# Attention's four engine queues written in another order, in a two-layer transformer kernel on one core

## What is computed

```python
def _L0_attn_ref(x, Wq, Wk, Wv, Wo, gn_weight, gn_bias):       # 8 heads of width 16
    qT, kT, vT = (proj(Wq), proj(Wk), proj(Wv))
    def step(S, qkv_t):
        q_t, k_t, v_t = qkv_t
        S = g * S + k_t[..., :, None] * v_t[..., None, :]      # g: one decay for each head
        y_t = jnp.einsum('bhde,bhd->bhe', S, q_t)
        return (S, y_t)
    ...
    out = (out - mean) * jax.lax.rsqrt(var + EPS)              # group norm over time and head width
    out = out.reshape(B, L, D) * gn_weight + gn_bias
    return out @ Wo.T

h = _layernorm(x, axis=-1) * (1 + ca) + sa
x = x + ga * _L0_attn_ref(h, ...)
h = _layernorm(x, axis=-1) * (1 + cb) + sb
scores = jnp.einsum('BTC,CE->BTE', h, gate_w)                  # logits of the feed-forward's router
probs = jax.nn.softmax(scores, axis=-1)
```

## Time and profile before

| what | value |
|---|---|
| median of 3 runs | 1448.95 us (1447.45 to 1464.47) |
| the profiled execution's own time | 1469.19 us |
| its span, first to last instruction | 1467.0 us |
| PE busy | 1130.1 us (77% of the span) |
| DVE busy | 893.7 us (61%) |
| ACT busy | 687.8 us (47%) |
| POOL busy | 561.8 us (38%) |
| mean granted TensorE clock | 0.859 |

### The profile page before, as it was taken

One profiled execution on the slowest core, in us unless ns is written; L12 is line 12 of the kernel. 1 busy time (PEld: TensorE's weight loads), 2 busy tenths in 40 slices (PEclk: granted clock), 3 DMA queues, 4 the chain that ended last, 5 costly groups with the idle time before them and its releaser, 6 DMA issues. The chain is left out here.

```text
span 1467.0 us, 23954 instructions
## 1 busy us (share of the span) xinstructions
PE 1130.1 (77%) x6776; PEld 857.3 (58%) x6777; DVE 893.7 (61%) x1786; ACT 687.8 (47%) x1527; POOL 561.8 (38%) x882
## 2 busy tenths in 40 slices
PE   2887885689978688888888888883374799999860
PEld 1555554334448578777888877773243666666640
DVE  2355553711039599999999999993376633333327
ACT  1334432233324587888778887771241033333320
POOL 1000000300012277777877778770000155555540
PEclk9667775799989789999999999996555599999995
DMA  6000000011010200000000000002310011111115
GB/s 181 0 1 1 0 1 1 0 44 43 29 29 0 58 1 1 1 0 0 0 0 0 0 0 0 0 0 90 97 33 17 6 35 39 36 39 38 38 48 181
DMA packets 41607, 39.87 MB, mean 27 GB/s; under 512 B 4041, under 2 KB 37474, under 8 KB 41202
## 3 DMA queue, kind: packets, MB, share of 16 engines
q1 hardware_dynamic: 32466, 22.37, 5.2%
q0 software_dynamic: 4608, 9.45, 2.3%
q10 hardware_dynamic: 4496, 7.60, 1.5%
HBM read 30.44 MB, written 8.96 MB: 27 GB/s over the span
## 5 line engine op out<-in xcount | busy, mean ns | idle before, releaser
L1181 DVE TENSOR_TENSOR_SCAN s_hs<-s_dA,bank 128x1024 f32<-128x1024 f32 x128 | 291.9, 2280 | 10.2 <-PE bank L1532 10.1
L1409 POOL TENSOR_SCALAR s_dbuT<-s_dtuT,s_BT 128x256 f32<-128x256 f32 x512 | 239.9, 492 | 11.0 <-ACT s_dtuT L1264 8.8
L1292 ACT ACTIVATE s_dA<-s_dt,aneg 128x255 f32<-128x255 f32 x512 | 213.6, 498 | 0.6 <-DVE s_hs L1181 0.4
L1982 POOL DMA_INDIRECT x_xg<-hf_rows,x_src x72 | 69.7, 968 | 236.9 <-issue 170.6
L1532 PE MATMUL bank<-const,s_dbuT 128*128 128x128 f32 x1024 | 139.7, 282 | 26.0 <-POOL s_dbuT L1409 26.0
L1189 DVE TENSOR_TENSOR s_hc<-s_hs,bank 128x1024 f32<-128x1024 f32 x128 | 156.1, 1220 | 5.2 <-PE bank L1520 0.9
L2022 PE MATMUL bank<-w,x_xT 128*128 x288 | 128.4, 569 | 19.0 <-ACT x_xT L2064 16.3
L1550 PE MATMUL bank<-const,s_hc 128*128 128x128 f32 x1024 | 138.0, 280 | 2.2 <-DVE s_hc L1189 2.2
L1532 PEld LDWEIGHTS bank<-const,s_dbuT 128*128 128x128 f32 x1024 | 119.8, 145 | 32.7 <-issue 26.3
L1550 PEld LDWEIGHTS bank<-const,s_hc 128*128 128x128 f32 x1024 | 120.7, 145 | 2.4 <-DVE s_hc L1189 2.4
L2060 ACT ACTIVATE x_a<-bank 128x448 f32<-128x448 f32 x72 | 39.1, 543 | 161.6 <-PE bank L2022 156.7
(11 more groups left out here) (301 smaller groups left out, 2273.6 us busy)
## 6 DMA issues: line engine op xcount, KB each, us to landing
w<-in_w SPq DMA_DIRECT2D x16, 256.0 KB, 3.1
o_yr<-y_rows SPq DMA_DIRECT2D x8, 512.0 KB, 3.9
w<-in_w ACTq DMA_DIRECT2D x1, 3584.0 KB, 13.3
x_res<-in_x SPq DMA_DIRECT2D x4, 512.0 KB
gate<-gates_d SPq DMA_DIRECT2D x2, 1024.0 KB, 5.6
s_gate<-gates_d SPq DMA_DIRECT2D x2, 1024.0 KB, 7.4
hf_rows<-r_rows SPq DMA_DIRECT2D x8, 256.0 KB, 2.2
out<-o_o ACTq DMA_DIRECT2D x8, 256.0 KB, 2.4
```

The source lines that it names most:

```text
L1181: dve.tensor_tensor_scan(flat(hs[:, j % 2]), flat(dA[:, j % RING]), bDbu[j % 2], 0.0, ALU.mult, ALU.add).then_inc(S["scanned"], 1)
L1292: ins = act.activation(dA[:, j % RING, h, n, 1:], dt[:, k, h, 1:], ACT.Exp, scale=m.aneg[:, h, 2 * j + n:2 * j + n + 1])
L1409: ins = pool.tensor_scalar(dbuT[:, j % RING, c, n, :], dtuT[:, k, c, :], BT[:, k, c, 2 * j + n:2 * j + n + 1], 1.0, ALU.mult, ALU.mult)
L1982: pool.indirect_dma_start(xg[k][:], None, m.hf_rows[:, :], bass.IndirectOffsetOnAxis(ap=src[k][:, 0:1], axis=0)).then_inc(S["rows"][k], 16)
```

## The change

Nothing is added to or taken from the arithmetic. The calls on PE, DVE and ACT stand in another order, and some are cut so that their parts can stand apart. `scores` and `masks` take a range of tiles: PE issues tiles 0-1, 2-3, 4-5, 6 and 7 with other steps between them, DVE masks 0, 1-2, 3-4, 5-6 and 7. On PE, queries now come before keys, and `values` after `output`. On ACT, `normalise` stands before `values`, which ends the round, `second_modulate` before `group_norm`, and queries and keys after it. On DVE, `layer_norm`, `group_variance`, `group_statistics` and `residual` are cut in two. `vp` gets a second buffer, so `values` of pair n waits only for the result of pair n - 2. `logits` waits in addition until the group means of n3 have been copied out of the bank that both use.

Most of the diff moves calls; this is the part that isn't plain order:

```diff
-        vp = sb("vp", [P, 2, Q, D])
+        vp = sb("vp", [P, 2, 2, Q, D])
...
-            def masks(n, k):
-                for j in range(4):
-                    i = 4 * k + j
+            def masks(n, first, end):
+                for i in range(first, end):
+                    k, j = divmod(i, 4)
...
-            def values(n):
+            def values(n, w):
                 act.wait_ge(S["v_ps"], n + 1)
                 act.activation(v0[:], bP[:, :].rearrange("p (s c d) -> p s c d", s=2, c=NCH)[:, :, 0, :], ACT.Copy)\
                     .then_inc(S["v_sb"], 1)
-                if later(n):
-                    act.wait_ge(S["y_ps"], n)
+                if not (isinstance(n, int) and n < 2):
+                    act.wait_ge(S["y_ps"], n - 1)
...
-            def scores(n, k, w):
-                if k == 0:
+            def scores(n, w, first, end):
+                if first == 0:
                     pe.wait_ge(S["k_sb"], n + 1)
                     pe.wait_ge(S["qm"], 2 * n + 2)
-                for j in range(4):
-                    i = 4 * k + j
+                for i in range(first, end):
+                    k, j = divmod(i, 4)
...
-            def logits(n):
+            def logits(n, n3):
                 pe.wait_ge(S["h2"], 2 * n + 2)
+                if n3 is not None:
+                    pe.wait_ge(S["g_own"], 3 * n3 + 1)
```

More of the change, by code:

```diff
@@ L431, in body @@
                 if n2 is not None:
+                    masks(n2, 0, 1)
+                if n3 is not None:
+                    group_squares(n3)
+                if n2 is not None:
+                    masks(n2, 1, 3)
+                if n3 is not None:
+                    group_mean(n3)
+                if n2 is not None:
                     state_blocks(n2)
-                    masks(n2, 0)
                 if n3 is not None:
                     group_variance(n3)
+                if n2 is not None:
+                    masks(n2, 3, 5)
+                if n3 is not None:
+                    group_affine(n3)
                 if n0 is not None:
                     layer_norm(n0)
+                if n2 is not None:
+                    masks(n2, 5, 7)
+                if n0 is not None:
+                    layer_moments(n0)
+                if n2 is not None:
+                    masks(n2, 7, 8)
+                if n4 is not None:
+                    softmax_shift(n4)
+                if n1 is not None:
+                    queries_on(n1, 1 - odd)
                 if n3 is not None:
-                    group_affine(n3)
-                if n2 is not None:
-                    masks(n2, 1)
+                    residual(n3)
                 if n0 is not None:
                     layer_shift(n0)
-                if n1 is not None:
-                    queries_on(n1, 1 - odd)
+                if n3 is not None:
+                    second_statistics(n3)
                 if n4 is not None:
-                    softmax_shift(n4)
-                if n3 is not None:
-                    residual(n3)
+                    softmax(n4)
                 if n1 is not None:
                     keys_on(n1)
-                if n4 is not None:
-                    softmax(n4)
                 if n3 is not None:
@@ L518, in keys_and_queries, with keys @@
                         .then_inc(S["qm"], 1)
-            def values(n):
+            def keys(n, w):
+                act.wait_ge(S["k_ps"], n + 1)
+                act.activation(kT[:, w], pairs_of(bP), ACT.Copy).then_inc(S["k_sb"], 1)
+            def values(n, w):
                 act.wait_ge(S["v_ps"], n + 1)
@@ L578, in body @@
                     group_rstd(n3)
-                if n1 is not None:
-                    keys_and_queries(n1, 1 - odd)
+                if n4 is not None:
+                    second_modulate(n4)
                 if n3 is not None:
                     group_norm(n3)
+                if n1 is not None:
+                    queries(n1, 1 - odd)
+                    keys(n1, 1 - odd)
                 if n0 is not None:
@@ L585, in body @@
                 if n4 is not None:
-                    second_modulate(n4)
-                if n1 is not None:
-                    values(n1)
+                    exponentials(n4)
                 if n0 is not None:
                     normalise(n0)
-                if n4 is not None:
-                    exponentials(n4)
                 if n3 is not None:
                     second_rstd(n3)
+                if n1 is not None:
+                    values(n1, 1 - odd)
             rounds(act, body)
@@ L638, in group_means, with queries, keys @@
                     .then_inc(S["g_ps"], 1)
-            def keys_and_queries(n):
-                hf = flat(hT[:])
+            def queries(n):
                 pe.wait_ge(S["h"], 2 * n + 2)
-                pe.matmul(bP[:, :], m.wk, hf, start=True, stop=True).then_inc(S["k_ps"], 1)
                 if later(n):
                     pe.wait_ge(S["state"], n)
-                pe.matmul(bQ[:, :], m.wq, hf, start=True, stop=True).then_inc(S["q_ps"], 1)
+                pe.matmul(bQ[:, :], m.wq, flat(hT[:]), start=True, stop=True).then_inc(S["q_ps"], 1)
+            def keys(n):
+                pe.matmul(bP[:, :], m.wk, flat(hT[:]), start=True, stop=True).then_inc(S["k_ps"], 1)
             def values(n):
@@ L706, in body @@
                 if n2 is not None:
+                    scores(n2, odd,  0,  2)
                     states(n2)
-                if n2 is not None:
-                    scores(n2, 0, odd)
+                    scores(n2, odd,  2,  4)
                 if n3 is not None:
                     group_means(n3)
+                if n2 is not None:
+                    scores(n2, odd,  4,  6)
                 if n4 is not None:
@@ L714, in body @@
                 if n1 is not None:
-                    keys_and_queries(n1)
+                    queries(n1)
+                    keys(n1)
                 if n2 is not None:
-                    scores(n2, 1, odd)
-                if n1 is not None:
-                    values(n1)
+                    scores(n2, odd,  6,  7)
                 if n4 is not None:
-                    logits(n4)
+                    logits(n4, n3)
+                if n2 is not None:
+                    scores(n2, odd,  7,  8)
                 if n3 is not None:
@@ L724, in body @@
                 if n1 is not None:
+                    values(n1)
                     first_keys(n1)
                 if n2 is not None:
-                    result(n2, 0, odd, n3)
-                    result(n2, 1, odd, n3)
+                    result(n2, 0,  odd,  n3)
+                    result(n2, 1,  odd,  n3)
             rounds(pe, body)
```

30 lines of the change are left out of this document (16 added, 14 removed).

## The result

The changed kernel takes 1418.13 us (median of 4, 1415.9 to 1422.73) against 1450.03 us (median of 4). The medians differ by 31.9 us; the ratio of the two kernels' runs is 0.9745, 95% interval 0.9706 to 0.9784, which is 37 us less (31 to 43). The forecast was 22.5 us. The profiled execution took 1422.73 us.

What follows compares the result with a forecast made beforehand. TensorE was taken as nearest to a bound in the attention phase, with waits between its work. Gains of 32.9 us less 10.5 paid gave about 22.5 us, 1448.95 to 1426.5 us; range 1404 to 1446.

Steps and rivals of the forecast that it cites:

- rival 2: Attention phase: clock rises to 0.84 from 0.72 as idling goes, another 23 us, 1403 to 1404 us; chance 0.20.
- The boundary, 15.4 us: Seven round boundaries: second vp buffer and earlier xn end TensorE's waits for xn; xn ready 2 us early, 15.4 us gained.
- Scores in pieces: Mask waits before tiles 3 and 7: other steps stand between, so 12.7 of 15.1 us are gained.
- att: TensorE's waits for att: values, first_keys ahead of the result cover its 0.76 us, so 3.1 us go.
- round 10: Last round, without a result: h2T goes first instead of behind ynT and starts earlier, 1.7 us gained.
- the 0.3 us a round that was left for tile 3: Tile 3's wait for mask 0: judged close, so 0.3 us left in each of 8 rounds.
- Rival 1: Round boundary: VectorE comes late, waits before tile 3 and the result remain; gain 10 us, 1439 us; chance 0.18.
- What the pieces cost, 9 + 1.5 us: Rounds 4 to 9: six more score groups at 1.5 us, 9 us; entering and leaving three more blocks per round, 1.5.
- The base: Whole kernel: gain subtracted unscaled from 1448.95 us, though the profiled execution stood 20.2 us above the median.
- Its own signs: Changed profile: xn and vp waits gone, rounds 5 to 7 near 21 us; wrong if phase clock moves 0.06 or more.
- Rival 3: Attention phase: more single tiles lower the clock; at 0.55 the kernel is slower, 1458 us; chance 0.10.

Runs made afterwards that it cites:

- the filled gap: Kernel before, with two added float32 matmuls of 512 columns in TensorE's gap ahead of the turn's wait for xn, from pair 2 on: ratio 0.9937.
- xn first alone: Kernel before, one buffer of vp, with only ScalarE's normalise moved ahead of values: ratio 0.9924.
- the square: Four kernels, boundary old or freed, scores in two blocks or pieces: before 1, before with two vp buffers 0.9788, changed with old boundary 1.0024, changed 0.9745.
- undoing one group in six rounds: Changed kernel with score tiles 6 and 7 joined ahead of logits: ratio 0.9582.
- in three blocks: Changed kernel with PE's scores as tiles 0-2, 3-5 and 6-7 instead of five pieces: 1388.39 us, ratio 0.9555.
- the changed kernel with the old boundary: Changed kernel with one buffer of vp and ScalarE's values, normalise, exponentials in their old order, so xn waits for the result: ratio 1.0024.

## Why the prediction was right, and where it was too small

The time lies in the range, and the gain is 1.4 times the 22.5 us of the forecast by the medians (31.9 us) and 1.6 times by the ratio (37 us). The prediction was right in what it gained and wrong in what it paid. It counted 32.9 us of waits, and 34.7 us of idling went (49.2 to 14.5). It let TensorE's work grow by 10.5 us, and since the time fell by 32 to 37 us, the work as a whole stayed as long as it was. A gain in clock that the sum doesn't have paid for the pieces. The time is in the range's lower half, where room was left for rival 2.

- **The boundary, 15.4 us.** Right as a wait: 15.2 us of the waits for `xn` go (33.0 to 17.8), and `xn` is ready 2.2 us early, where 2 was worked out. As time the free boundary is 31 to 40 us. The step that failed is the sum's silent assumption that TensorE's own work keeps its length. The text had that as rival 2 with 0.20, and worked it as idling against clock; the filled gap shows that this exists, at about 9 us. Why freeing the boundary gives more than that, and xn first alone little or nothing beyond its waits, is open. The reason given to it, the second buffer, was needed only in the old order.
- **Scores in pieces, att and round 10, 12.7 + 3.1 + 1.7 = 17.5 us.** Right: 18.0 us of idling, in both rows of the square. All 15.1 before scores went as idle time, and the 0.3 us a round that was left for tile 3 is there, inside the blocks (0.2 for tile 3, 0.1 for tile 5). Of `att` 2.2 of 3.1 went. Rival 1 did not happen.
- **What the pieces cost, 9 + 1.5 us.** Right for the work itself: in round 5 the blocks that wait for nothing take 1.07 and 1.06 us from start to start, against the 1.05 taken. As time the square gives 7 to 12 us with the new boundary and 21 with the old, so the size isn't settled. But undoing one group in six rounds was worth 24 us (14 to 34), not 6 to 12, and no idle time went with it. Its price isn't only its own length. That the rest is the clock follows from this and from the whole program's clock; why a single tile lowers it isn't shown. So the pieces and the rest of the new order are worth between nothing and 11 us net, and in three blocks nearly the same waits go at a profit.
- **The base.** The first profile of the kernel before had the low clock, 0.72, and a later one 0.78. Its time, 20 us above the median, was the sign: between the two profiles lie 18.6 us (1469.19 and 1450.60), and 13.2 of them in this phase. Read from the later profile, the clock of the phase rose hardly at all between before and changed (0.78 to 0.78 or 0.81): freeing the boundary raised it and the pieces lowered it.
- **Its own signs.** The waits went as listed, and rounds 5 to 7 took 17.42, 19.02 and 20.67 us at 0.90, 0.82 and 0.75, where 21 at 0.75 was said. But "the phase's clock moves by 0.06 or more" stood there as a sign of being wrong, and it moved from 0.72 to 0.78. By rival 2's price that is 11 us, and 22.5 + 11 comes near the measured gain; since the kernel before has 0.78 in its later profile, this can be chance.
- **Rival 3** was right in kind: the changed kernel with the old boundary has 0.70, the lowest of all, and alone among the experiments is no faster than the kernel before (1.0024, equal within the noise).

## What to carry to other kernels

Where TensorE is the bound, count what each cut of its stream adds in groups that can't run side by side: on this kernel a block of one 32-row tile costs what a block of three does (1.13 and 1.15 us), as long as no tile of it waits. Cut a block only as often as a buffer forces it; three tiles to a block for three banks idled 16.4 us where five pieces idled 14.5, at 28 us less. Look for waits inside merged rows too: a block that takes longer than its like at the same clock, 1.79 us against 1.15, holds one. And read more than one profile before a phase's busy time is taken for the kernel's: idling agreed to 0.1 us between executions, busy time only to 13 and 6.

## What was not expected of the hardware

The granted clock fell without any idling. In the changed kernel rounds 5 and 8 have the same TensorE work (round 8 lacks only pair n0, which is none of TensorE's) and it is busy for all of both: 17.42 us at 0.90, 23.89 us at 0.64. (The waits inside blocks, about 0.3 us a round, are the same in both.) The filled gap shows that idling counts too. What decides between 1.2 and 2.4 GHz in a stretch of mixed small matmuls wasn't settled, and the same program met both, from one execution to the next and from one round to the next.
